# A graph network on one core: first-half ranks computed a stage earlier, keep ranks by quarters, and a halved first chain in the attention

## The chip, the cores and the metric

The program runs on one core of a Trainium2 chip. The metric is device time in microseconds (us). A core has TensorE (PE; its weight loads are PEld), VectorE (DVE), ScalarE (ACT), GpSimd (POOL) and SyncE (SP), whose queue issues the bulk DMAs. The engines run their own instruction streams and meet at semaphores.

## The reference

Eight graphs of 1024 nodes with 128 features pass through four residual blocks: an attention, a three-layer network on a thinned adjacency, a normalised graph convolution and a mask convolution. Each begins with a layer norm and a relu. Cut to what matters here:

```python
h = jnp.maximum(_layernorm(x, axis=-1), 0.0)
# attention
Wh = jnp.einsum('bnc,dc->bnd', h, W_w) + W_b
s = si[:, :, None] + sj[:, None, :] + a_b
e = jnp.exp(s) * A
h_prime = jnp.einsum('bij,bjc->bic', e / jnp.sum(e, axis=2, keepdims=True), h)
...
# thinning: row by row, a removal also clears the symmetric entry
def step(carry, n):
    row = jnp.take(carry, n, axis=0)
    nbi = row.astype(jnp.int32)
    num = jnp.sum(nbi)
    sf = jnp.where(num > T_DIL, (num + K_DIL - 1) // K_DIL, 1)
    rank = jnp.cumsum(nbi)
    rm = row & (rank % sf == 0)
    ...
    carry = carry.at[n].set(row & keep)
    carry = carry.at[:, n].set(carry[:, n] & keep)
...
# one layer on the thinned adjacency
agg = jnp.einsum('bij,bjd->bid', adj, x) / deg
out = agg @ Wr + x @ Wx + b
return out / nrm * mf[..., None]
```

## The kernel before, in words

A graph's nodes are cut into NB = 8 blocks of P = 128; HALF is 512 columns, one PSUM bank of f32. The stages follow one another with a barrier between: attention, removal, the fused stage, two layers, the convolution and the last block. The change touches the first three.

**Attention** (`attention_phase`, L173). Graph order is 1 to 7, then 0. Per graph: norm statistics on DVE (`mean`), the root on POOL (`root`), the scaled relu on ACT (`normalised`, L122), two score sums per block on DVE (`score_sums`, L415), the exponentials on ACT (`scores`, L363), the right-hand side on POOL (`right_hand_side`, L284) and 64 f32 products on PE (`attention`, L333), which waits for the right-hand side and for all four chunks of the adjacency. SP loads x of the first graph, waits for it, loads x of the second, then four 1 MB chunks per graph (L234). ACT issues five small constants itself; DVE waits for them first of all. ACT also sums every column of the adjacency (`column_sums`), DVE writes the bits into T8 (`bits`).

**Removal** (`removal_phase`, L488). All eight graphs go together, block by block. In block nb DVE runs 2 to 4 rounds (`parameters`, `hits`), each answered by PE (`lost`), then sets the removal parameters kd and kb (`far_parameters`). Beside these rounds the previous block is finished: PE forms its far ranks (`far_codes`, L629) in a ring of three PSUM slots, ACT turns them into distances (`distances`, L775 and L778), DVE compares them (`staying`, L907), PE and ACT form the current rows (`current`, L643, L787), PE counts them (`far_counts`, L586). DVE can't begin the next block before these counts (`pl_summed`, L926). After the last block ACT norms the first graph (L122), then forms the last distances, and DVE ends the stage with them (L911).

**Fused stage** (`fuse_phase`, L977). T8 is now final, and each graph is treated in 8 steps. A piece (nb, lo, hi) is up to 512 columns left of block nb's diagonal; a graph has 12. Per piece PE makes ranks (`ranks`, L1082: one fp8 matmul per block jb, from jb's column to the piece's end, so 512, 384, 256 and 128 columns for a full piece), ACT the distance to the bias kb (or kbhigh in the second half) (`distances`, L1192), DVE the removal bits into the buffer low (`removals`, L1271). Two rank banks alternate. With the bits, PE makes a mask per half row block (`masks`), DVE applies it to the adjacency (`masked_rows`, L1283), and PE adds the layer's f32 products (`sums`, L1143). In a step PE does the masks of graph b, the ranks of graph b+1, small projections, and the sums of the step before. The ranks of graph 0 come before the first mask, all 12 pieces one after the other.

## Time and profile before

| what | us |
|---|---|
| three runs | 1225.6, 1227.59, 1229.71; median 1227.59 |
| the profiled execution | 1230.29 |
| its span, first to last instruction | 1228.5 |
| PE busy | 1132.6 (92% of the span) |
| DVE busy | 768.1 (63%) |
| ACT busy | 603.2 (49%) |

The stages by their first and last instructions: attention ends with PE's products at 142.9 us, removal with DVE at 323.7 us, the fused stage begins on PE at 324.6 us. A timeline row gives start, duration, engine, line, the tile written and read, the count, and in brackets the idle time before it with what ended it. "issue" is a gap that no wait explains. PEclk is the clock that TensorE was granted, 1.00 being the upper level.

### The profile page before, as it was taken

The numbers are of one execution on the slowest core, as the hardware profiler recorded it, in microseconds if no ns is written. First come the engines' busy times: TensorE is split into PE (matmuls) and PEld (weight loads), VectorE is DVE, ScalarE is ACT, GpSimd is POOL, SyncE is SP. The second block draws the span as 40 slices with busy tenths as digits, with TensorE's granted clock in tenths as the row PEclk, the third lists the DMA queues.
The fourth block names the chain that finished last, engine by engine and source line by source line (L and its number), as shares of the span: only waits on it lengthen the run. The fifth ranks groups of instructions, "written<-read, shape, count | busy, mean of one in ns | idle before, by whom it ended". The sixth has DMA issues, their size and how long they took to land. (4 is left out here: it accounts for less than half of the span.)

```text
span 1228.5 us, 26838 instructions
## 1 busy us (share of the span) xinstructions
PE 1132.6 (92%) x9677; PEld 928.4 (76%) x9693; DVE 768.1 (63%) x2813; ACT 603.2 (49%) x1557; POOL 114.3 (9%) x129
## 2 busy tenths in 40 slices
PE   3999899998599999999899999999999899996998
PEld 3999866665388889889699999799999555543554
DVE  5899578677467777766434545435364655646973
ACT  3888557676746666664323334223435523314351
POOL 3333000000000000000000000213132101100000
PEclk9999889876699999999899999999999999998999
DMA  8977212110336677773246663157575355634911
GB/s 330 315 284 282 63 25 35 24 30 14 142 134 263 257 275 275 275 270 143 86 172 245 270 226 136 53 197 302 193 301 196 133 218 210 257 137 190 397 47 52
DMA packets 105513, 228.92 MB, mean 186 GB/s; under 512 B 34528, under 2 KB 53152, under 8 KB 105376
## 3 DMA queue, kind: packets, MB, share of 16 engines
q1 hardware_dynamic: 104656, 227.07, 50.0%
q8 instruction: 80, 1.31, 0.4%
q14 instruction: 57, 0.47, 0.1%
q10 hardware_dynamic: 720, 0.07, 0.0%
HBM read 185.70 MB, written 37.75 MB: 182 GB/s over the span
## 5 line engine op out<-in xcount | busy, mean ns | idle before, releaser
L1488 PE MATMUL lay_acc<-lay_z,k_keepadj 128*128 128x128 f32 x1024 | 117.0, 275 | 0.0
L1488 PE MATMUL lay_acc<-lay_z,k_otheradj 128*128 128x128 f32 x1024 | 117.0, 275 | 0.0
L1488 PEld LDWEIGHTS lay_acc<-lay_z,k_keepadj 128*128 128x128 f32 x1024 | 115.6, 192 | 0.0
L1488 PEld LDWEIGHTS lay_acc<-lay_z,k_otheradj 128*128 128x128 f32 x1024 | 115.6, 192 | 0.0
L1538 ACT ACTIVATE lay_junk<-lay_o 128x128 bf16<-128x128 f32 x128 | 37.7, 295 | 123.1 <-DVEq L1633 123.1
L1608 DVE TENSOR_TENSOR lay_o<-lay_ring,k_vec 128x512 f32<-128x512 f32 x32 | 22.1, 692 | 104.2 <-PE lay_ring L1481 104.2
L333 PE MATMUL att_acc<-att_rhs,att_adjT 128*128 128x130 f32 x512 | 60.8, 283 | 13.3 <-POOLq L285 12.3
L1587 POOL TENSOR_TENSOR lay_bl<-k_vec,k_mask 128x256 f32<-128x256 f32 x32 | 21.0, 655 | 553.6 <-DVEq L1623 549.7
L333 PEld LDWEIGHTS att_acc<-att_rhs,att_adjT 128*128 128x128 f32 x512 | 60.2, 198 | 13.8 <-POOLq L285 12.4
L1546 ACT ACTIVATE lay_o<-lay_o,lay_nrm 128x128 f32<-128x128 f32 x128 | 39.4, 388 | 54.4 <-DVE lay_nrm L1644 54.4
L1192 ACT ACTIVATE fuse_dist<-fuse_prank,k_kb 128x512 f16<-128x512 f32 (+2 forms) x64 | 38.9, 607 | 51.7 <-PE fuse_prank L1082 49.5
L1143 PE MATMUL fuse_acc<-fuse_z,k_otheradj 128*128 128x129 f32 x512 | 61.9, 275 | 0.0
L1143 PE MATMUL fuse_acc<-fuse_z,k_keepadj 128*128 128x129 f32 x512 | 61.9, 275 | 0.0
L333 PE MATMUL att_acc<-att_rhs,k_keepadj 128*128 128x130 f32 x512 | 58.1, 276 | 1.9 <-issue 1.9
L1143 PEld LDWEIGHTS fuse_acc<-fuse_z,k_keepadj 128*128 128x128 f32 x512 | 59.4, 192 | 0.0
L1143 PEld LDWEIGHTS fuse_acc<-fuse_z,k_otheradj 128*128 128x128 f32 x512 | 59.4, 192 | 0.0
L333 PEld LDWEIGHTS att_acc<-att_rhs,k_keepadj 128*128 128x128 f32 x512 | 57.5, 191 | 2.5 <-issue 2.5
L1283 DVE SCALAR_TENSOR_TENSOR k_otheradj<-fuse_pmask,k_otheradj 128x512 f32<-128x512 f32 x64 | 44.1, 689 | 21.5 <-PE fuse_pmask L1104 13.0
L1760 PE MATMUL gcn_agg<-k_keepadj,gcn_hs 128*128 128x512 f32 x128 | 56.4, 593 | 1.2 <-DVE k_keepadj L1857 1.2
L1082 PE MATMUL fuse_prank<-k_fore,k_T 128*128 128x128 fp8e5 (+3 forms) x288 | 46.5, 289 | 11.8 <-PEq L140 9.7
L1283 DVE SCALAR_TENSOR_TENSOR k_keepadj<-fuse_pmask,k_keepadj 128x512 f32<-128x512 f32 x64 | 44.1, 689 | 20.8 <-PE fuse_pmask L1104 10.8
L1760 PE MATMUL gcn_agg<-k_otheradj,gcn_hs 128*128 128x512 f32 x128 | 56.3, 592 | 0.0
(295 smaller groups left out, 2535.8 us busy)
## 6 DMA issues: line engine op xcount, KB each, us to landing
k_keepadj<-in_adj_cols SPq DMA_DIRECT2D x28, 1024.0 KB, 9.0
k_keepadj<-keptT SPq DMA_DIRECT2D x12, 2048.0 KB, 11.0
k_otheradj<-keptT SPq DMA_DIRECT2D x12, 2048.0 KB, 11.1
att_adjT<-in_adj_cols SPq DMA_DIRECT2D x16, 1024.0 KB, 8.1
k_otheradj<-in_adj_cols SPq DMA_DIRECT2D x16, 1024.0 KB, 10.3
keptT<-k_keepadj SPq DMA_DIRECT2D x16, 1024.0 KB, 4.6
keptT<-k_otheradj SPq DMA_DIRECT2D x16, 1024.0 KB, 4.6
lay_rowf<-in_adj_rows SPq DMA_DIRECT2D x32, 512.0 KB, 14.6
```

The costliest lines, as they stand in the source:

```text
L333: mm = t.matmul(acc[n % NA][:, e // 2, e % 2, 0:W], adjT[i % 2][:, jb, ib * P:(ib + 1) * P], rhs[i % 2][:, jb, 0:W], start=(jb == 0), stop ...
L1082: mm = t.matmul(prank[n % NR][:, a - lo:hi - lo], T8[:, b, jb, nb * P:(nb + 1) * P], K["fore8"][:, a - jb * P:hi - jb * P], start=(jb == f ...
L1143: mm = t.matmul(acc_tile(ib)[:, 0:ZW], adjT[b % 2][:, jb, ib * P:(ib + 1) * P], zz[:, jb, :], start=(jb == 0 and ib % 3 == 0), stop=(jb == ...
L1192: a.activation(dist[n % NR][:, 0:hi - lo], prank[n % NR][:, 0:hi - lo], ACT.Abs, bias=bias)
L1283: v.scalar_tensor_tensor(rows, pmask[n % NM][:], -0.5, rows, ALU.is_lt, ALU.mult)
L1488: mm = t.matmul(acc[i % 2][k][:, ib % HB, :], adjT[i % 2][:, jb, ib * P:(ib + 1) * P], zz[i % 2][:, jb, :], start=(jb == 0), stop=(jb == N ...
L1538: a.activation(junk[:, ib, :], o[i % 2][:, ib, :], ACT.Square, accum_out=nrm[:, 0, ib:ib + 1])
L1546: last = a.activation(o[i % 2][:, ib, :], o[i % 2][:, ib, :], ACT.Relu, scale=nrm[:, 4, ib:ib + 1])
L1587: g.tensor_tensor(bl[:], along_tiles(K["vec"][:, V_BL, :], 2), along_features(K["mask"][:, tile:tile + 2], D), ALU.mult)
L1608: v.tensor_tensor(o[i % 2][:, half * HB:(half + 1) * HB, :], ring[n % NS][:], along_tiles(K["vec"][:, V_B1 + layer, :], HB), ALU.add)
L1760: mm = t.matmul(agg[b % 2][:, sl], hs[b % 2][:, jb, :], adjT[b % 2][:, jb, sl], start=(jb == 0), stop=(jb == NB - 1))
```

## The change

- **Attention, first graph.** x comes in two halves with a semaphore each. SP then waits for the small constants, not for x, and x of the second graph goes behind the first graph's four adjacency chunks. DVE takes the statistics of the first half ahead of the constants. ACT signals the relu after four of eight blocks, and DVE's score sums begin there. The exponentials come ahead of the first column sums, and the first right-hand side is made by DVE.
- **Removal.** The pieces of graph 0 in the first half of blocks 0 to 6 (seven of its 12) are made here: `near_ranks` on PE at the end of a block, `near_distances` on ACT behind the current rows, `near_removals` on DVE two blocks later in round 0. `far_counts` keeps more partial counts. The norm of the first graph moves on ACT from the stage's end into block 0. 14 idle matmuls stand at PE's end.
- **Fused stage.** Each piece is ranked by quarters of 256 columns, each counted from its own start, so the widths are 256, 128, 256, 128. Each quarter has its own bias, and ACT does one activation per quarter. Graph 0 has five pieces left ahead of the first mask.
- **Memory.** low is kept for the whole program, and buffers of other stages are laid over it.

```diff
-                load_x(0)
-                sp.wait_ge(x_loaded[0], 16)
-                load_x(1)
+                for half in range(2):
+                    ts = slice(half * NB // 2, (half + 1) * NB // 2)
+                    sp.dma_start(x_rows(0)[:, ts, :], graph(A["x"], order[0])[:, ts, :]).then_inc(x_first[half], 16)
+                sp.wait_ge(small_loaded, 16 * 5)
                 for i in range(2):
                     for c in range(NC):
                         load_adjacency(i, c)
-                    load_x(i + 2)
-                for i in range(4, B):
+                    load_x(i + 1)
+                for i in range(3, B):
                     load_x(i)
                 sp.dma_start(maski[:], A["nodemask"].rearrange("b (t p) -> (b t) p", p=P)).then_inc(mask_loaded, 16)
...
-                root(0)
                 for i in range(B):
-                    right_hand_side(i)
-                    if i == 0:
-                        root(1)
-                    if 0 < i < B - 1:
-                        root(i + 1)
+                    root(i)
+                    if i > 0:
+                        right_hand_side(i)
...
+                normalised_first()
+                act.drain()
+                scores(0)
+                column_sums(0, 0)
...
-                    dve.wait_ge(h_ready, i + 1)
+                    dve.wait_ge(h_ready if i > 0 else half_ready, i + 1)
...
+                        if i == 0 and t == NB // 2:
+                            dve.wait_ge(h_ready, 1)
...
+                def first_rows():
+                    x = x_rows(0)
+                    for half in range(2):
+                        dve.wait_ge(x_first[half], 16)
+                        if half == 1:
+                            both_columns()
+                        for t in range(half * NB // 2, (half + 1) * NB // 2):
+                            v.bn_stats(w["part"][:, t, :], x[:, t, :])
+                    dve.drain()
+                    for t in range(NB):
+                        last = v.bn_aggr(w["pair"][:, t, :], w["part"][:, t, :])
+                    last.then_inc(w["mean_ready"], 1)
+
+                def first_right_hand_side():
+                    dve.wait_ge(exp_ready, 1)
+                    v.tensor_copy(rhs[0][:, :, D], E[0][:])
+                    v.tensor_tensor(rhs[0][:, :, 0:D], h[0][:], along_features(E[0][:], D), ALU.mult)
+                    dve.drain().then_inc(rhs_ready, 1)
...
+                def near_ranks(nb):
+
+                    o = take()
+                    top = min(HALF, (nb + 1) * P)
+                    for jb in range(min(nb, HALF // P - 1) + 1):
+                        mm = t.matmul(o[:, jb * P:top], T8[:, 0, jb, nb * P:(nb + 1) * P], K["fore8"][:, 0:top - jb * P],
+                                      start=(jb == 0), stop=(jb == min(nb, HALF // P - 1)))
+                    mm.then_inc(ring_ready, 1)
...
-                        if nb < LOW:
-                            for jb in range(LOW, NB):
-                                add(pl[:, NB + jb - LOW, b:b + 1], T8[:, b, nb, jb * P:(jb + 1) * P], K["ones8"][:, 0:1])
+                        beyond_pair = 2 * (nb // 2) + 2
+                        for jb in range(beyond_pair, NB):
+                            slot_of = LOWSLOT + {2: 0, 4: 6, 6: 10}[beyond_pair] + jb - beyond_pair
+                            add(pl[:, slot_of, b:b + 1], T8[:, b, nb, jb * P:(jb + 1) * P], K["ones8"][:, 0:1])
...
+                    if not more:
+                        keep_busy(t, K, take()[:, 0:HALF], 14)
...
+                def near_distances(nb):
+
+                    if nb >= 2:
+                        act.wait_ge(near_read, nb - 1)
+                    o = take()
+                    top = min(HALF, (nb + 1) * P)
+                    a.activation(near_dist[nb % 2][:, 0:top], o[:, 0:top], ACT.Abs, bias=K["kb"][:, nb:nb + 1])
+                    act.drain().then_inc(near_ready, 1)
+                    act.sem_inc(ring_free, 1)
...
+                        near_distances(prev)
+                    else:
+                        norm_apply(nc, act, lambda t: K["X"][:, t, :], K["h"][:], row, 0, first_h)
                     if more:
                         distances(nb, first)
-                norm_apply(nc, act, lambda t: K["X"][:, t, :], K["h"][:], row, 0, first_h)
                 distances(NB - 1, range(B))
...
+                def near_removals(nb):
+
+                    dve.wait_ge(near_ready, nb + 1)
+                    top, c0 = min(HALF, (nb + 1) * P), low_columns(nb)
+                    v.tensor_scalar(K["low"][:, c0:c0 + top], near_dist[nb % 2][:, 0:top], K["kd"][:, nb:nb + 1], None, ALU.is_equal)\
+                        .then_inc(near_read, 1)
...
+                        if nb > 1 and k == 0:
+                            near_removals(nb - 2)
...
-                high = K["kb"][:].rearrange("p (b t) -> p t b", t=NB)[:, LOW:NB, :]
-                v.tensor_tensor(K["kbhigh"][:], high, lowcount[:], ALU.add)
+                kb = K["kb"][:].rearrange("p (b t) -> p t b", t=NB)
+                sides = K["rdeg"][:].rearrange("p (b t) -> p t b", t=NB)
+                v.tensor_tensor(lowcount[:, 6:10, :], lowcount[:, 6:10, :], lowcount[:, 2:6, :], ALU.add)
+                v.tensor_tensor(sides[:, 0:6, :], kb[:, 2:8, :], lowcount[:, 0:6, :], ALU.add)
+                dve.drain()
+                v.tensor_tensor(lowcount[:, 10:12, :], lowcount[:, 10:12, :], lowcount[:, 8:10, :], ALU.add)
+                v.tensor_tensor(K["kbhigh"][:], kb[:, LOW:NB, :], lowcount[:, 6:10, :], ALU.add)
+                dve.drain()
+                v.tensor_tensor(sides[:, 6:8, :], kb[:, 6:8, :], lowcount[:, 10:12, :], ALU.add)
+                near_removals(NB - 2)
                 staying(NB - 1, range(B))
...
+    early = [q for q in range(NP) if pieces[q][0] < NB - 1 and pieces[q][1] == 0]
+    left = [q for q in range(NP) if q not in early]
...
+        def of_block(b, nb):
+            return [q for q in (left if b == 0 else range(NP)) if pieces[q][0] == nb]
+
+        def piece_number(b, q):
+            return left.index(q) if b == 0 else b * NP + q - len(early)
+
+        def quarters(lo, hi):
+            return [(q0, min(q0 + HALF // 2, hi)) for q0 in range(lo, hi, HALF // 2)]
+
+        def offset(b, nb, q0):
+
+            t = b * NB + nb
+            if q0 == HALF:
+                return K["kbhigh"][:, nb - NB // 2, b:b + 1]
+            return {0: K["kb"][:, t:t + 1], HALF // 2: K["rdeg"][:, t - 2:t - 1] if nb >= 2 else None,
+                    3 * HALF // 2: K["rdeg"][:, t:t + 1]}[q0]
 
         def acc_tile(ib):
...
-                        for jb in range(first_jb, last_jb + 1):
-                            a = max(jb * P, lo)
-                            mm = t.matmul(prank[n % NR][:, a - lo:hi - lo], T8[:, b, jb, nb * P:(nb + 1) * P],
-                                          K["fore8"][:, a - jb * P:hi - jb * P], start=(jb == first_jb), stop=(jb == last_jb))
+                        for q0, q1 in quarters(lo, hi):
+                            for jb in range(q0 // P, q1 // P):
+                                mm = t.matmul(prank[n % NR][:, jb * P - lo:q1 - lo], T8[:, b, jb, nb * P:(nb + 1) * P],
+                                              K["fore8"][:, 0:q1 - jb * P], start=(jb * P == q0), stop=((jb + 1) * P == q1),
+                                              skip_group_check=True)
...
+                ranks(0, 4)
                 side_work("turn_h", 0, 0)
-                ranks(0, 1)
+                ranks(0, 5)
                 side_work("turn_h", 0, 1)
-                ranks(0, 2)
-                ranks(0, 3)
+                ranks(0, 6)
+                ranks(0, 7)
                 side_work("z", 0, 0)
-                for nb in range(4, NB):
-                    ranks(0, nb)
                 for b in range(B + 1):
                     if b < B:
...
                         tile = b * NB + nb
-                        bias = K["kb"][:, tile:tile + 1] if lo == 0 else K["kbhigh"][:, nb - NB // 2, b:b + 1]
-                        a.activation(dist[n % NR][:, 0:hi - lo], prank[n % NR][:, 0:hi - lo], ACT.Abs, bias=bias)
+                        for q0, q1 in quarters(lo, hi):
+                            a.activation(dist[n % NR][:, q0 - lo:q1 - lo], prank[n % NR][:, q0 - lo:q1 - lo], ACT.Abs,
+                                         bias=offset(b, nb, q0))
                         act.drain().then_inc(dist_ready, 1)
 
                 def side_copy(kind, b, half):
```

In all three of the following places names are those of the program; k_low is the buffer low, att_sj the scores, att_rhs the right-hand side. First DVE at the start of the attention, before:

```order
L445 COPY att_abc<-att_acol 128x128 x2
L92 BN_STATS att_n_part<-k_X 128x6 x8
L95 BN_AGGR att_n_pair<-att_n_part 128x2 x8
L400 SCALAR_TENSOR_TENSOR att_n_stat<-att_n_stat,att_n_pair 128x8
L450 COPY att_av<-att_pset 128x256
L451 COPY att_ac<-att_pset 128x2
L453 TENSOR_TENSOR att_ac<-att_ac,att_ab 128x1
L415 SCALAR_TENSOR_TENSOR att_prod,att_sj<-att_h,att_av 128x128 x16
L92 BN_STATS att_n_part<-k_X 128x6 x8
```

and in the change:

```order
L440 BN_STATS att_n_part<-k_X 128x6 x4
L430 COPY att_abc<-att_acol 128x128 x2
L440 BN_STATS att_n_part<-k_X 128x6 x4
L443 BN_AGGR att_n_pair<-att_n_part 128x2 x8
L406 SCALAR_TENSOR_TENSOR att_n_stat<-att_n_stat,att_n_pair 128x8
L479 COPY att_av<-att_pset 128x256
L480 COPY att_ac<-att_pset 128x2
L482 TENSOR_TENSOR att_ac<-att_ac,att_ab 128x1
L423 SCALAR_TENSOR_TENSOR k_low,att_sj<-att_h,att_av 128x128 x16
L448 COPY att_rhs<-att_E 128x8
L449 TENSOR_TENSOR att_rhs<-att_h,att_E 128x8x128
L92 BN_STATS att_n_part<-k_X 128x6 x8
```

Four of the statistics stand ahead of the copies of the constants, and the right-hand side stands ahead of the second graph's statistics. Next ACT from the end of the removal stage to the first distances of the fused stage, before:

```order
L787 ACTIVATE k_T<-rem_ring,rem_minus 128x256 x8
L122 ACTIVATE k_h<-k_X,rem_n_stat 128x128 x8
L775 ACTIVATE rem_dist<-rem_cand,rem_shift 128x128 x8
L561 UNCONDITIONAL_BRANCH
L1176 UNCONDITIONAL_BRANCH
L1231 ACTIVATE fuse_prime<-k_eps 128x1
L1192 ACTIVATE fuse_dist<-fuse_prank,k_kb 128x128
L1202 ACTIVATE fuse_hT<-fuse_misc 128x512
L1192 ACTIVATE fuse_dist<-fuse_prank,k_kb 128x256
L1202 ACTIVATE fuse_hT<-fuse_misc 128x512
L1192 ACTIVATE fuse_dist<-fuse_prank,k_kb 128x384
L1192 ACTIVATE fuse_dist<-fuse_prank,k_kb 128x512
```

and in the change:

```order
L837 ACTIVATE k_T<-rem_ring,rem_minus 128x256 x8
L847 ACTIVATE rem_near_dist<-rem_ring,k_kb 128x512
L825 ACTIVATE rem_dist<-rem_cand,rem_shift 128x128 x8
...
L1285 ACTIVATE fuse_dist<-fuse_prank,k_kbhigh 128x128
L1296 ACTIVATE fuse_hT<-fuse_misc 128x512
L1285 ACTIVATE fuse_dist<-fuse_prank,k_kbhigh 128x256
L1296 ACTIVATE fuse_hT<-fuse_misc 128x512
L1285 ACTIVATE fuse_dist<-fuse_prank,k_kbhigh 128x256
L1285 ACTIVATE fuse_dist<-fuse_prank,k_rdeg 128x128
L1285 ACTIVATE fuse_dist<-fuse_prank,k_kb 128x256
L1285 ACTIVATE fuse_dist<-fuse_prank,k_rdeg 128x256
```

The eight norm activations have left the end, one distance has come in their place, and the fused stage begins with the second-half piece of block 4; k_rdeg holds the biases of the second and fourth quarter. Last PE in step 7 of a graph, where two full pieces are ranked, before:

```order
L1082 MATMUL fuse_prank<-k_fore,k_T 128x512
L1082 MATMUL fuse_prank<-k_fore,k_T 128x384
L1082 MATMUL fuse_prank<-k_fore,k_T 128x256
L1082 MATMUL fuse_prank<-k_fore,k_T 128x128
L1082 MATMUL fuse_prank<-k_fore,k_T 128x512
L1082 MATMUL fuse_prank<-k_fore,k_T 128x384
L1082 MATMUL fuse_prank<-k_fore,k_T 128x256
L1082 MATMUL fuse_prank<-k_fore,k_T 128x128
L1130 MATMUL fuse_misc<-k_Wr,fuse_hT 128x128 x4
```

and in the change:

```order
L1176 MATMUL fuse_prank<-k_fore,k_T 128x256
L1176 MATMUL fuse_prank<-k_fore,k_T 128x128
L1176 MATMUL fuse_prank<-k_fore,k_T 128x256
L1176 MATMUL fuse_prank<-k_fore,k_T 128x128
L1176 MATMUL fuse_prank<-k_fore,k_T 128x256
L1176 MATMUL fuse_prank<-k_fore,k_T 128x128
L1176 MATMUL fuse_prank<-k_fore,k_T 128x256
L1176 MATMUL fuse_prank<-k_fore,k_T 128x128
L1225 MATMUL fuse_misc<-k_Wr,fuse_hT 128x128 x4
```

The count stays at eight matmuls, the columns go from 2560 to 1536.

## Rows read from the trace of the kernel before

**Rows 1.** the profile page, part 1: busy us (share of the span), instructions

```profile
PE 1132.6 (92%) x9677; PEld 928.4 (76%) x9693; DVE 768.1 (63%) x2813; ACT 603.2 (49%) x1557; POOL 114.3 (9%) x129
```

**Rows 2.** window of 32 us: busy of PE, PEld, DVE, ACT, POOL, then PEclk

```profile
377.00:409.00 32.00, 31.63 (x305) 28.67 (x306) 23.54 (x67) 20.70 (x57) 0.00 (x0) 1.00 0.69 260
```

**Rows 3.** timeline of PE: start us, us, engine, line, what; fused stage, step 7

```profile
394.97 0.39 PE L1107 MATMUL fuse_pmask<-k_minus,k_T 128*128 128x128 fp8e5 x4
395.19 0.22 PE L1095 MATMUL fuse_pmask<-k_T,k_minus 128*128 128x128 fp8e5 x1
...
395.69 1.25 PE L1082 MATMUL fuse_prank<-k_fore,k_T 128*128 128x512 fp8e5 x8
396.78 0.44 PE L1130 MATMUL fuse_misc<-k_Wr,fuse_hT 128*128 128x128 f32 x2
```

**Rows 4.** waits in total, times, longest (us): PE in 345 to 600 us

```profile
PE fuse_pmask L1095 <- issue: 1.9, 7, 0.3
```

**Rows 5.** groups by line and shape, ACT: xcount, then busy, mean ns, idle

```profile
L1192 ACT ACTIVATE fuse_dist<-fuse_prank,k_kb 128x512 f16<-128x512 f32 x35 | 24.1, 688 | 42.8 <-PE fuse_prank L1082 42.8
...
L1192 ACT ACTIVATE fuse_dist<-fuse_prank,k_kbhigh 128x256 f16<-128x256 f32 x7 | 3.3, 474 | 1.1 <-issue 1.1
```

**Rows 6.** timeline of PE, start of the fused stage

```profile
324.56 0.27 PE L1082 MATMUL fuse_prank<-k_fore,k_T 128*128 128x128 fp8e5 x1 [9.74 <-PEq L140]
...
338.24 0.39 PE L1095 MATMUL fuse_pmask<-k_T,k_minus 128*128 128x512 fp8e5 x1 [1.63 <-DVE fuse_low L1271]
```

**Rows 7.** window (columns as in rows 2), entry of the fused stage

```profile
324.00:329.00 5.00, 4.04 (x18) 2.84 (x19) 0.58 (x3) 2.82 (x6) 0.11 (x1) 0.50 0.67 220
```

**Rows 8.** timeline of ACT, end of the removal stage

```profile
316.28 3.18 ACT L122 ACTIVATE k_h<-k_X,rem_n_stat 128x128 f32<-128x128 f32 x8 [0.26 <-issue]
319.37 3.90 ACT L775 ACTIVATE rem_dist<-rem_cand,rem_shift 128x128 f16<-128x128 f16 x8
```

**Rows 9.** timeline of DVE, the same place

```profile
319.81 0.35 DVE L911 SCALAR_TENSOR_TENSOR k_T<-rem_dist,k_kd,k_T 128x128 fp8e5<-128x128 f16 x1 [3.70 <-ACTq L780]
```

**Rows 10.** timeline of PE, attention's first products

```profile
20.52 17.25 PE L333 MATMUL att_acc<-att_rhs,att_adjT 128*128 128x130 f32 x128 [12.29 <-POOLq L285]
38.23 14.53 PE L333 MATMUL att_acc<-att_rhs,k_keepadj 128*128 128x130 f32 x128 [0.45 <-issue]
```

**Rows 11.** timeline of all engines, start of attention

```profile
5.61 2.11 SPq L234 DMA_DIRECT2D att_adjT<-in_adj_cols  x4
5.95 0.36 DVE L445 COPY att_abc<-att_acol 128x128 f32<-128x128 f32 x2 [5.95 <-DMA att_ab<-in_L_gnn_a_b]
6.23 1.64 DVE L92 BATCH_NORM_STATS2 att_n_part<-k_X 128x6 f32<-128x128 f32 x8
...
12.61 1.63 ACT L122 ACTIVATE att_h<-k_X,att_n_stat 128x128 f32<-128x128 f32 x4
14.27 0.29 DVE L415 SCALAR_TENSOR_TENSOR att_prod<-att_h,att_av 128x128 bf16<-128x128 f32 x1 [2.71 <-ACT att_h L122]
...
18.52 1.90 POOL L284 TENSOR_TENSOR att_rhs<-att_h,att_E 128x1024 f32<-128x1024 f32 x1
...
30.47 1.90 POOL L284 TENSOR_TENSOR att_rhs<-att_h,att_E 128x1024 f32<-128x1024 f32 x1
```

**Rows 12.** DMA, 0 to 60 us in 40 slices

```profile
GB/s 0 73 313 10 144 372 407 415 423 426 415 426 349 378 404 404 410 407 421 401 326 293 295 296 289 290 301 425 423 401 421 421 412 101 0 19 246 412 421 418
```

**Rows 13.** waits of DVE, removal stage, 166 to 300 us

```profile
DVE rem_stays L907 <- ACTq L780: 7.8, 13, 1.3
DVE rem_w L926 <- PEq L732: 7.2, 4, 2.4
```

**Rows 14.** timeline of PE, removal stage, end of block 4

```profile
262.57 0.49 PE L586 MATMUL rem_pl<-k_ones,k_T 128*128 128x1 fp8e5 x14
263.69 0.33 PE L586 MATMUL rem_pl<-k_ones,k_T 128*128 128x1 fp8e5 x7 [0.62 <-ACTq L789]
```

**Rows 15.** groups by line and shape, DVE in 345 to 600 us

```profile
L1271 DVE TENSOR_SCALAR fuse_low<-fuse_dist,k_kd 128x512 bf16<-128x512 f16 x42 | 14.8, 353 | 9.3 <-ACTq L1193 6.5
```

120 lines of the change are left out of this document (63 added, 57 removed).

## The prediction

> **What bounds the kernel now.** I read the page first: PE is busy for 92% of the span, DVE for 63%, ACT for 49% [rows 1]. That share is a mean over stages, so each stage the change touches was read for what ends its waits last.
>
> *Fused stage.* In a window of 32 us, one graph's work, PE is busy for 31.6, DVE for 23.5 and ACT for 20.7, at granted clock 1.00 [rows 2]. In all of 345 to 600 us PE waits 1.9 us in front of the masks [rows 4]. So what PE sheds is shed from the stage. Its matmuls go by their columns: in step 7 the eight rank matmuls, 2 x (512+384+256+128) = 2560 columns, stand from 395.69 to 396.78, 1.09 us, and four of 128 columns with changing weights from 394.97 to 395.19, 0.055 each [rows 3]. That is 0.0533 per 128 columns at the upper level, 2.4 GHz.
>
> *Entry of the fused stage.* From PE's first rank to the first mask pass 338.24 - 324.56 = 13.7 us, and the mask was released by DVE's removal bits, the end of the chain PE, ACT, DVE over 12 pieces [rows 6]. Until 329 PE is granted 0.50, 1.2 GHz [rows 7].
>
> *End of removal.* ACT norms for 3.18 us from 316.28 and only then starts the last distances, at 319.37 [rows 8]; DVE had waited 3.70 us for them [rows 9].
>
> *Inside removal* no engine is full. DVE waits 7.8 us for ACT's distances and 7.2 for PE's counts [rows 13]. Here the change adds work to all three.
>
> *Start of attention.* PE waits 12.29 us for POOL's right-hand side, until 20.52 [rows 10]. The chain there is constants, statistics, root, relu, score sums, exponentials, right-hand side [rows 11]. The next product starts at 38.23, after a gap of 0.45 that no other engine ends [rows 10]; from there PE is the bound, so an earlier first product moves the stage's end.
>
> **The change, part by part.**
>
> *Ranks by quarters.* A piece of m blocks had m(m+1)/2 units of 128 columns. Full pieces (six per graph) go from 10 units to 6, pieces of three (two) from 6 to 4, the rest stay. 80 units become 52, so 28 x 0.0533 = 1.49 us per graph, and 7 x 1.49 = 10.4 us for graphs 1 to 7, whose ranks stand in PE's full steps. Graph 0 is in the next term. For it ACT pays one more activation in eight pieces: 512 columns take 688 ns, 256 take 474 [rows 5], so 2 x 474 - 688 = 260 ns, 2.1 us per graph: ACT goes from 20.7 to 22.8 of then 30.5 us. Work of PE hides it; if that cover failed, up to 2.1 x 7 = 15 us would come back, more than the gain. I take it as hidden: two rank banks give a piece a whole step to be read, and a step has 3.8 us. DVE's work stays. Gain 10.4; bounds 0 (ACT's latency eats all of it) and 10.4.
>
> The Trainium skill, "TensorE: Matmul & The Clock Gate", section "Back-to-back issue gap", puts a sustained stream of weight load and matmul at about 81 ns per matmul of 128 columns, since the load counts too. That would speak against quarters: the 128-column matmuls of a graph go from 12 to 20, and the gain would be an estimated 8 x 0.027 x 7 = 1.5 us smaller. The trace has 55 ns for the same pair [rows 3], so the trace decides, and the sum goes by columns.
>
> *Graph 0's first halves made early.* Of 12 pieces 5 remain ahead of the first mask: 128, 256, 384, 512 and 512 columns. ACT's line there, by the durations of rows 5 (107 ns per 128 columns above 260): 0.37 + 0.47 + 0.84 + 0.95 + 0.95 = 3.6 us, and the two copies of hT, each taken as a full activation, 0.69: 5.0 together. Eight gaps of 0.16 to 0.2 between them, from the idle before such groups, 7 x 0.16 = 1.1 in total [rows 5], add 1.4; start 0.3, the last removal and its hand-over 0.5. Sum 7.2 against 13.7: gain 6.5. The end norm root and z copy now stand behind the last distance, not ahead of it. Bounds: 5 (if PE's half clock makes it wait between) and 8.
>
> *The norm off the end.* It goes to block 0, where ACT has nothing until the first parameters. At the end ACT runs one near distance, 0.69 + 0.18, in its place: 3.18 - 0.87 = 2.3 us earlier. DVE's five small sums and a near removal fit in the 3.70 it waited [rows 9]. Gain 2.3; bounds 1.5 and 3.1. What is late next is the same chain of eight distances. The 14 matmuls of PE behind it are 14 x 0.213 at full and 0.427 at half clock, 3 to 6 us, starting near 315.5, so they end by 321.5, about when DVE ends; at worst they cost 0.5. They keep PE occupied up to the stage change.
>
> *What removal pays.* Seven near ranks, distances and removals, and 64 more one-column counts. DVE: a 512-wide removal takes 353 ns [rows 15], narrower ones less, six of them in round 0 of blocks 2 to 7, 1.6 to 1.9 us; nothing of DVE's own hides them, only its waits for ACT. PE: the counts and the near ranks stand ahead of the signal on which DVE starts a block. 14 counts take 0.49 [rows 14], 0.03 each. At the end of blocks 1 and 2, where PE comes last, ten counts and one or three short ranks cost about 0.45 each, 0.9. Later PE waits 0.62 there for ACT's rows [rows 14], which covers four rank matmuls (10 units, 0.53). ACT: near distances of 0.87 delay the next block's distances, which wait for PE's far ranks anyway early on; for blocks 5 and 6 I count 1.4. Queued behind ACT's near distance are three far distances, and DVE's `staying` waits for those. Sum 3.9, less 0.8 where DVE's removal falls into a wait for ACT: 3.1 lost. Bounds: 0, since more work on PE may hold its clock up, and all additions in a row: 1.9 for DVE, 4.7 for ACT (0.55 + 0.65 + 0.76 + 3 x 0.87 rounded up for hand-overs), 40 units at half clock 4.3, 64 counts 1.8: 12.7.
>
> *Attention.* Four of eight statistics go ahead of the constants, half of 1.64: 0.8. Score sums start after four of eight relus: the last four take 1.63 [rows 11], so 1.6. The right-hand side takes POOL 1.90 [rows 11]; on DVE, not shown here, it is bound by three widths of rows 15 (f16 in) and POOL's own 1.9; I take 1.2, gain 0.6. The chain gives 3.0. But PE also needs the last adjacency chunk. Counted by slices of 1.5 us [rows 12], 5.2 MB have arrived by about 18.5. Without the 0.5 MB of the second x, at 415 GB/s, this is 1.3 earlier, and 0.35 later because SP now starts at 5.95 and not at 5.61 [rows 11]. So the chunk lands at 17.6 and the rest of the hand-over makes 18.0: gain 2.5. The second x arrives at about 19, which delays DVE by about 1 us; the second product, wanted at 35.7, had its right-hand side at 32.4 [rows 11], so 2 us of cover are left. Bounds 0.5 and 3.2. The warm-up of PE (17.25 against 14.53 [rows 10]) stays.
>
> *Sum.* -10.4 - 6.5 - 2.3 + 3.1 - 2.5 = -18.6 us. The profiled execution is 1230.3 (span 1228.5 and 1.8 around it), so 1211.7; it lies 2.7 above the median of the runs. Against the median 1227.6 this is 1209.0, the forecast.
>
> **The rivals.**
>
> *A: the quarters' gain stays on paper.* ACT's longer chain reaches the graph's boundary, where the first mask waits for all bits of the next graph. For: DVE already waits for ACT there 6.5 us in full pieces [rows 15]. Against: ACT waits for PE 42.8 us in front of these activations [rows 5], and behind the last ranks PE still has 16 sums. If half of the 10.4 is lost, the time is 1214; if all, 1219.
>
> *B: removal pays in full.* ACT is last in most blocks and the three-slot ring passes each near rank's delay on. For: the waits of DVE [rows 13]. Against: those of PE for ACT [rows 14]. 12.7 instead of 3.1 gives 1218.
>
> *C: slower.* The near rank takes a ring slot at each block's end, PE stands blocked until ACT frees one, and its granted clock stays at 0.50 for the rest of removal, as it is at the stage's end. It decides from about 22 us lost there, 3.2 per block, nearly twice what all additions come to in a block at their upper bound (12.7 over seven). The time would be 1231. Nothing in the rows shows such a wait.
>
> *D: the early pieces don't shorten the entry*, because the transposes and projections alone take it. They take PE and ACT together under 5 us, so at most 2 us are lost: 1211. Within the forecast's range.
>
> **How the numbers follow.** Forecast with D 0.74, A 0.10, B 0.12, C 0.04. The forecast's own bounds (attention 0.5 to 3.2, entry 5 to 8, end 1.5 to 3.1, removal 0 to 5) give 1203 to 1215. The range reaches into A and B: 1202 to 1218. This kernel's runs tell about 0.3%, 3.7 us, from no change. Faster by more than that 0.94, within it 0.03, slower 0.03.
>
> **What would show it.** Right: a graph's stretch in the fused stage falls from about 32 us to 30.6 with PE still without waits; the first mask comes 7 us behind the first rank; the last distances begin right behind the near distance; PE's first product starts near 18; removal between attention's end and its own last distance is about 3 us longer. Wrong: PE waits for removal bits at graph boundaries (A), DVE's waits for counts and distances above 20 us (B), or a mean clock in removal clearly below before (C).

## The result, and the profile after

| | before | after |
|---|---|---|
| median of the timed runs, us | 1226.99 (1225.60 to 1229.71) | 1211.94 (1209.21 to 1214.89) |
| ratio, 95% interval | | 0.9871, 0.9848 to 0.9894 |
| profiled execution, us | 1230.29 | 1211.67 |
| its span, mean granted clock | 1228.5, 0.954 | 1209.9, 0.967 |

The change saves 15.1 us of the median, 18.6 of the profiled execution. The forecast was 1209.0 with a range of 1202 to 1218: the time lies inside, 2.9 above the forecast. The sum of the prediction was -18.6, exactly what the two profiles differ by. That is luck, since its terms were not right, and their errors cancel. One run of one experiment, 1913.7 us at a granted clock of 0.558 in the kernel with one activation, is left out everywhere below. This is how the spans divide, each mark read from the same instruction in both profiles:

| stretch | before | after | difference | in the sum |
|---|---|---|---|---|
| start to the end of attention's products | 142.9 | 145.9 | +3.0 | -2.5 |
| from there to the fused stage's first rank | 181.7 | 178.6 | -3.1 | +0.8 (3.1 - 2.3) |
| first rank to first mask | 13.7 | 6.6 | -7.1 | -6.5 |
| first mask to the 26 filling matmuls behind the last graph | 250.1 | 241.4 | -8.7 | -10.4 |
| from there to the end | 640.2 | 637.5 | -2.7 | 0 |

One term was close (the entry), one was a fifth too large, two had the wrong sign, and one was missing.

The page of the changed kernel, part 1 (busy us, share of the span, instructions); before in [rows 1]:

```profile
PE 1118.8 (92%) x9755; PEld 925.1 (76%) x9771; DVE 769.9 (64%) x2819; ACT 612.2 (51%) x1616; POOL 112.9 (9%) x127
```

**Attention.** The timeline of PE (start, us, engine, line, operation; in brackets what it idled for), the changed kernel; before in [rows 10]:

```profile
18.36 15.99 PE L331 MATMUL att_acc<-att_rhs,att_adjT 128*128 128x130 f32 x128 [10.24 <-DMA att_adjT<-in_adj_cols]
34.71 14.53 PE L331 MATMUL att_acc<-att_rhs,k_keepadj 128*128 128x130 f32 x128 [0.36 <-POOLq L286]
53.52 17.15 PE L331 MATMUL att_acc<-att_rhs,att_adjT 128*128 128x130 f32 x128 [4.28 <-DMA att_adjT<-in_adj_cols]
71.14 14.53 PE L331 MATMUL att_acc<-att_rhs,k_keepadj 128*128 128x130 f32 x128 [0.47 <-issue]
```

The first product starts 2.2 us earlier than before, about as forecast (18.4; forecast near 18), and the second 3.5 earlier. Then the third waits 4.28 us for its adjacency and, after the pause, takes 17.15 instead of 14.53. In the wait the mean granted clock is 0.83, in the first 2.5 us of the product 0.50. The third product starts at 53.52, 0.3 behind the 53.23 of the kernel before, so the early start is given back by the wait, and 2.6 of the 3.0 us lost are the slower product. DVE's statistics, ACT's relus and SP's issues of the changed kernel show why:

```profile
20.02 1.65 DVE L92 BATCH_NORM_STATS2 att_n_part<-k_X 128x6 f32<-128x128 f32 x8 [2.90 <-DMA k_X<-in_x]
33.20 1.64 DVE L92 BATCH_NORM_STATS2 att_n_part<-k_X 128x6 f32<-128x128 f32 x8 [1.62 <-DMA k_X<-in_x]
```

```profile
40.07 3.19 ACT L122 ACTIVATE att_h<-k_X,att_n_stat 128x128 f32<-128x128 f32 x8 [3.20 <-DVE att_n_stat L406]
43.16 1.04 ACT L378 ACTIVATE k_low<-att_adjT 128x1024 bf16<-128x1024 f32 x1
```

```profile
17.59 18.91 SPq L230 DMA_DIRECT2D k_X<-in_x  x6
36.54 2.02 SPq L247 DMA_DIRECT2D att_maski<-in_nodemask  x1
38.69 7.29 SPq L234 DMA_DIRECT2D att_adjT<-in_adj_cols  x4
```

The second graph's x is now behind 4 MB of adjacency, so DVE's second statistics start at 20.02 instead of 17.95; the third's wait again. ACT, which takes graphs in turn, does the third graph's relus at 40.07 (before: 36.83) and only behind them the column sums of the last chunk of the first graph's buffer, from 43.16. On these SP waits before it issues the last chunk of the third graph's adjacency into that buffer, at 45.61 instead of 42.67.

This delay is real, but it is not all that PE waits for. The rate of the DMA in the changed kernel, 30 to 60 us in 40 slices of 0.75 us:

```profile
GB/s 324 287 295 295 292 289 279 298 292 293 289 272 304 273 205 382 378 404 421 410 404 404 426 421 377 399 421 399 317 366 377 333 229 333 410 399 437 415 410 273
```

From 41.25 to 51 us it never pauses: while the last chunk wasn't issued, the three ahead of it were still moving. It landed 7.7 us behind its issue, at 53.3. In the kernel before it landed 8.7 us behind its issue, at 51.4, and PE, still in its second product until 52.76, didn't see it. So a third product could not have started much before 51.4 even with the old order, and an earlier start of PE can give at most about 2 us there. The prediction has no term for this.

**End of removal, and entry of the fused stage.** ACT and PE there, the changed kernel; before in [rows 6, 8]:

```profile
318.32 0.69 ACT L847 ACTIVATE rem_near_dist<-rem_ring,k_kb 128x512 f16<-128x512 f32 x1 [0.37 <-PE rem_ring L689]
319.24 3.92 ACT L825 ACTIVATE rem_dist<-rem_cand,rem_shift 128x128 f16<-128x128 f16 x8 [0.24 <-issue]
```

```profile
318.14 3.26 PE L1459 MATMUL rem_ring<-k_fore,k_ident 128*128 128x512 fp8e5 x14
324.47 0.22 PE L1176 MATMUL fuse_prank<-k_fore,k_T 128*128 128x128 fp8e5 x1 [3.07 <-PEq L140]
328.61 0.82 PE L1176 MATMUL fuse_prank<-k_fore,k_T 128*128 128x256 fp8e5 x4 [0.55 <-ACTq L1287]
331.04 0.63 PE L1190 MATMUL fuse_pmask<-k_T,k_minus 128*128 128x512 fp8e5 x1
```

The last distances stand right behind the near one, and the first mask comes 6.6 us behind the first rank with no wait of its own (before, 1.63).

**Fused stage.** A window of one graph, 30.8 us (columns as in [rows 2]), and the waits of PE in 345 to 570 us (engine, line, whom it waited for: total us, times, longest):

```profile
394.90:425.70 30.80, 30.44 (x307) 28.46 (x307) 23.72 (x67) 22.13 (x65) 0.00 (x0) 1.00 0.72 273
```

```profile
PE fuse_pmask L1190 <- issue: 2.0, 7, 0.3
PE fuse_misc L1223 <- ACT fuse_o L1322: 0.2, 1, 0.2
```

PE is still the bound, with waits as in [rows 4]; ACT went from 20.7 in 32 us to 22.1 in 30.8.

**Behind the fused stage**, in code that the change leaves as it is, PE gets its clock back sooner. Windows of 3 us (the number behind POOL is the granted clock) at the same place, 15 us behind the start of the filling matmuls, before and after:

```profile
603.30:606.30 3.00, 3.00 (x13) 2.35 (x12) 0.84 (x2) 0.00 (x0) 0.00 (x0) 0.50 0.97 388
```

```profile
587.40:590.40 3.00, 3.00 (x23) 2.50 (x22) 0.64 (x2) 0.78 (x2) 0.00 (x0) 0.90 1.02 401
```

At 0.50 (the 1.2 GHz level) 13 matmuls start, at 0.90 23. In windows of 1.5 us from the same start, the clock is back at 1.00 some 2.5 us sooner. The second layer begins (first 2 us) at 0.56 before and 1.00 after, the convolution at 0.50 and 1.00. The first layer is 1.1 us shorter, the second 0.8, the rest 0.8.

### The profile page after: what moved, and what is told of

Same layout as the page of the kernel before. It is cut to its first block and busy times, and to the rows that moved or that the text cites. A ratio compares the mean times of both kernels' runs of the same rounds, so it can differ in the third digit from the quotient of the medians.

```text
span 1209.9 us, 27058 instructions
## 1 busy us (share of the span) xinstructions
PE 1118.8 (92%) x9755; PEld 925.1 (76%) x9771; DVE 769.9 (64%) x2819; ACT 612.2 (51%) x1616; POOL 112.9 (9%) x127
## 5 line engine op out<-in xcount | busy, mean ns | idle before, releaser
L1701 DVE TENSOR_TENSOR lay_o<-lay_ring,k_vec 128x512 f32<-128x512 f32 x32 | 22.1, 692 | 102.4 <-PE lay_ring L1574 102.4
L331 PE MATMUL att_acc<-att_rhs,att_adjT 128*128 128x130 f32 x512 | 62.2, 287 | 15.1 <-DMA att_adjT<-in_adj_cols 14.5
L1680 POOL TENSOR_TENSOR k_low<-k_vec,k_mask 128x256 f32<-128x256 f32 x32 | 21.2, 664 | 535.4 <-DVEq L1716 531.9
L666 PE MATMUL rem_ring<-k_back,k_T 128*128 128x512 fp8e5 (+3 forms) x272 | 51.0, 350 | 2.9 <-ACTq L829 1.9
L2109 PE MATMUL l_agg<-k_T,k_low 128*128 128x512 fp8e5 x192 | 44.5, 394 | 9.4 <-PEq L140 9.4
```

What stands on the lines that cost most here:

```text
L331: mm = t.matmul(acc[n % NA][:, e // 2, e % 2, 0:W], adjT[i % 2][:, jb, ib * P:(ib + 1) * P], rhs[i % 2][:, jb, 0:W], start=(jb == 0), stop ...
L666: mm = t.matmul(o[:, lo - f0:top - f0], T8[:, b, mb, n0:n0 + P], K["back8"][:, u0:u0 + top - lo], start=(mb == NB - 1), stop=(mb == lo // P))
L1680: g.tensor_tensor(bl, along_tiles(K["vec"][:, V_BL, :], 2), along_features(K["mask"][:, tile:tile + 2], D), ALU.mult)
L1701: v.tensor_tensor(o[i % 2][:, half * HB:(half + 1) * HB, :], ring[n % NS][:], along_tiles(K["vec"][:, V_B1 + layer, :], HB), ALU.add)
L2109: mm = t.matmul(agg[b % 2][:, sl], parts[b % 2][:, q, jb, :], bits_of(b, jb)[:, sl], start=(jb == 0 and q == 0), stop=(jb == NB - 1 and q ...
```

## Experiments

Each set of runs has the kernel before beside it on the same chip (the sets were on different chips); the ratio is to that kernel, with its 95% interval in brackets, so between sets compare the ratios. The marks are of one profile each. "Removal" is the stretch from the end of attention's products to the first rank.

| kernel | median us | ratio | attention's end | removal | entry | fused |
|---|---|---|---|---|---|---|
| changed | 1211.9 | 0.9871 [0.9848, 0.9894] | 145.9 | 178.6 | 6.6 | 241.4 |
| changed, again | 1210.5 | 0.9861 [0.9839, 0.9883] | 145.2 | 178.7 | 6.6 | 241.3 |
| old attention | 1209.2 | 0.9859 [0.9839, 0.9880] | 142.0 | 179.0 | 6.7 | 240.7 |
| second x first | 1207.8 | 0.9848 [0.9826, 0.9870] | 142.0 | 179.5 | 6.8 | 241.0 |
| loads by need | 1208.3 | 0.9830 [0.9788, 0.9872] | 141.5 | 180.5 | 6.7 | 240.9 |
| both moves | 1208.9 | 0.9850 [0.9828, 0.9872] | 143.1 | 179.7 | 6.8 | 240.8 |
| whole ranks | 1221.3 | 0.9950 [0.9931, 0.9968] | 146.9 | 179.2 | 6.3 | 250.0 |
| one activation | 1211.1 | 0.9873 [0.9847, 0.9899] | 143.9 | 178.7 | 6.3 | 239.8 |
| norm only | 1223.0 | 0.9956 [0.9933, 0.9980] | 142.6 | 174.6 | 13.6 | 250.0 |
| no fill | 1211.7 | 0.9856 [0.9801, 0.9911] | 145.9 | 178.8 | 7.0 | 240.9 |
| no near pieces | 1209.7 | 0.9846 [0.9803, 0.9889] | 143.0 | 177.1 | 6.1 | 240.7 |
| norm at the end | 1214.4 | 0.9895 [0.9874, 0.9915] | 145.2 | 180.7 | 7.0 | 241.2 |
| before, again | 1230.9 (one run) | | 143.2 | 181.9 | 13.7 | 250.1 |

### Attention: the old stage

The changed kernel with the attention functions of the kernel before (buffers shared as in the changed one):

```diff
-                first_rows()
+                dve.wait_ge(small_loaded, 16 * 5)
+                for half in range(2):
+                    last = v.tensor_copy(abc[:, half, :], acol[:, half:half + 1].to_broadcast([P, P]))
+                last.then_inc(abc_ready, 1)
+                mean(0)
...
-                first_right_hand_side()
```

> The changed kernel with the attention stage of the kernel before. My theory: the new attention costs 3.0 us instead of gaining 2.5, because the second graph's x now lands behind 4 MB of adjacency, DVE's second statistics start 2 us late, and with them every step of the chain up to the adjacency chunks of the third graph. So PE ends the stage at 142.9 us as before (145.9 in the changed kernel), the third product starts without a wait and lasts 14.5, and the time falls by 3.0, to about 1209. Rival: the stage's end merely varied between the two profiles, and the new attention is a gain of 2: then the time is about 1214.

The stage ends at 142.0 and the median falls by 2.8 against the first set of the changed kernel, by 1.3 against the second. The ratios (0.9859 against 0.9871 and 0.9861) don't tell them apart; the stage's end does. PE's first and third products of this kernel:

```profile
20.59 16.38 PE L331 MATMUL att_acc<-att_rhs,att_adjT 128*128 128x130 f32 x128 [12.29 <-POOLq L283]
52.34 14.53 PE L331 MATMUL att_acc<-att_rhs,att_adjT 128*128 128x130 f32 x128 [0.48 <-DVEq L439]
```

With the first product 2.2 us later, the third starts 1.2 earlier. The changed kernel, profiled again, waits 3.30 us at its third product, which takes 16.18, and ends the stage at 145.2, as was expected of it. Over seven profiles with the new attention the stage ends between 143.0 and 146.9 (median 145.2), over four with the old one (the before kernels' included) between 142.0 and 143.2 (median 142.7). The ranges touch, and the medians are 2.5 apart: the new attention is a loss in most profiles, not in all. The one at 143.0 (no near pieces) tells where the loss sits:

```profile
53.27 14.53 PE L331 MATMUL att_acc<-att_rhs,att_adjT 128*128 128x130 f32 x128 [2.46 <-DMA att_adjT<-in_adj_cols]
```

It waits 2.46 us, the granted clock stays at 1.00, and the product takes 14.53. In the six others PE waited 2.89 to 4.48 us, the product took 16.18 to 17.29, and the stage ended at 143.9 or later. What is lost is the slower product.

### Attention: the second graph's x first

```diff
                 sp.wait_ge(small_loaded, 16 * 5)
+                load_x(1)
                 for i in range(2):
                     for c in range(NC):
                         load_adjacency(i, c)
-                    load_x(i + 1)
+                    load_x(i + 2)
```

> The changed kernel with one transfer moved: the second graph's x is issued ahead of the first adjacency. My theory (late x): the first product starts about 1 us later, at 19.4, the second right-hand side is ready by 33 and not 34.2, the third product starts at 51.5 to 52 with no wait for its adjacency and lasts 14.5, and the stage ends near 142; the time falls by 4, to about 1208. Rival (ACT's new order): the column sums come late because ACT now runs exponentials, column sums and relus of the second graph in another order, so the third product still waits some 4 us for its last chunk and the stage ends at 146 or 147: time 1212 to 1213.

DVE's second statistics and PE's products in it:

```profile
17.24 1.65 DVE L92 BATCH_NORM_STATS2 att_n_part<-k_X 128x6 f32<-128x128 f32 x8 [0.19 <-issue]
```

```profile
19.69 17.00 PE L332 MATMUL att_acc<-att_rhs,att_adjT 128*128 128x130 f32 x128 [11.65 <-DMA att_adjT<-in_adj_cols]
37.05 14.53 PE L332 MATMUL att_acc<-att_rhs,k_keepadj 128*128 128x130 f32 x128 [0.36 <-issue]
52.20 14.53 PE L332 MATMUL att_acc<-att_rhs,att_adjT 128*128 128x130 f32 x128 [0.62 <-DMA att_adjT<-in_adj_cols]
```

The wait for x is gone, the third product starts at 52.20 after 0.62 us, at full speed, and the stage ends at 142.0. ACT's order is the changed one, so that rival falls: the place of one 0.5 MB transfer decides. The time, 1207.8, is as expected.

The way there is not only the theory's. The wait of 4.28 us is 3.66 shorter. Of these, 2.34 come from PE, whose second product ends at 51.58 and not at 49.24, since the first one starts later and takes longer. Only 1.3 come from the adjacency: its last chunk is issued 4.2 us sooner, at 41.45, but lands 10.5 behind its issue, at 52.0.

### Attention: loads in the order of need

```diff
                 for i in range(2):
                     for c in range(NC):
                         load_adjacency(i, c)
-                    load_x(i + 1)
-                for i in range(3, B):
-                    load_x(i)
-                sp.dma_start(maski[:], ...)
+                    if i == 0:
+                        load_x(1)
+                        load_x(2)
+                load_x(3)
                 for i in range(2, B):
...
                         load_adjacency(i, c)
+                    if i + 2 < B:
+                        load_x(i + 2)
+                    if i == 2:
+                        sp.dma_start(maski[:], ...)
```

> The changed kernel with SP's loads in the order of need: x of the first two following graphs behind the first adjacency, x of the fourth behind the second, the rest and the node mask behind the third adjacency and later. The first product keeps its early start. My theory (what is late in the changed kernel is the third graph's adjacency, which SP issues only at 38.7 us, behind six loads of x and the mask, and whose last chunk waits for the late column sums): first product at 18.3, second at 34.8, third at about 50 without a cold clock, stage's end near 140, so 6 us earlier than the 145.9 of the changed kernel and 2 earlier than with the second x first; time about 1206. Rival: the order of SP's queue is worth nothing since the late x of the second graph alone sets the chain; then the third product still starts at 52 to 53.5, the end is 144 to 146 and the time 1210 to 1212.

```profile
18.23 16.31 PE L335 MATMUL att_acc<-att_rhs,att_adjT 128*128 128x130 f32 x128 [10.26 <-DMA att_adjT<-in_adj_cols]
35.07 14.56 PE L335 MATMUL att_acc<-att_rhs,k_keepadj 128*128 128x130 f32 x128 [0.54 <-POOLq L290]
50.20 14.55 PE L335 MATMUL att_acc<-att_rhs,att_adjT 128*128 128x130 f32 x128 [0.57 <-POOLq L290]
65.33 14.54 PE L335 MATMUL att_acc<-att_rhs,k_keepadj 128*128 128x130 f32 x128 [0.58 <-POOLq L290]
```

SP's row of this kernel for the third graph's adjacency starts at 34.61 instead of 38.69, and the third product at 50.20, as the theory said. Here the second x is still late, ACT's relus for the third graph come at 39.44 and the last chunk is issued at 44.98, nearly as late as in the changed kernel; yet it lands 5.0 us later: the three ahead of it had been moved by 44.5, where the DMA's rate falls to nothing. So the late column sums alone don't make the wait of 4.28 us; the place of this adjacency behind six loads of x and the mask has part in it. But the stage ends at 141.5, not 140, and the time is 1208.3, not 1206: five products now wait 0.54 to 0.58 for POOL's right-hand side, at a spacing of 15.1 us, and the last one 1.74, 4.5 us in all. DVE's late x had hidden behind the late adjacency; with that gone, the chain through DVE, ACT and POOL is the bound.

### Attention: both moves together

> The changed kernel with both moves of SP's loads: the second graph's x ahead of the first adjacency, and the later graphs' x and the mask behind the third adjacency. Theory (behind the third product DVE's period of 15.1 us per graph and PE's 15.0 leave nothing to gain): the first product starts at 19.5 to 19.7, the third at 51.8 to 52 without a wait, the stage ends at 141.5 to 142, and the time is 1207.5, 4.5 under the changed kernel and the same as either move alone. Rival (the two moves add): the stage ends at 140 and the time is 1205.5.

It is 1208.9, against 1210.5 for the changed kernel beside it; 1207.5 was expected. The moves don't add, as expected. The stage ended at 143.1, not 141.5 to 142: in this profile the first product waited for its adjacency until 20.88, 1.2 longer than in the kernel with one move, and everything behind kept this distance. The second x first, alone, is the version with the lowest median, 1207.8 us (0.9848); loads by need, at 1208.3, can't be told from it.

### Fused stage: ranks whole again

```diff
-                        for q0, q1 in quarters(lo, hi):
-                            for jb in range(q0 // P, q1 // P):
-                                mm = t.matmul(prank[n % NR][:, jb * P - lo:q1 - lo], ...
+                        for jb in range(lo // P, hi // P):
+                            mm = t.matmul(prank[n % NR][:, jb * P - lo:hi - lo], ...
...
-                        for q0, q1 in quarters(lo, hi):
-                            a.activation(dist[n % NR][:, q0 - lo:q1 - lo], ...
+                        a.activation(dist[n % NR][:, 0:hi - lo], ...
```

> The changed kernel with the fused stage's ranks whole again and one activation per piece (for the pieces from block 2 on in each half the second half then lacks the quarters' offset only if ranks were by quarters; here none is missing). My theory: PE's columns set the graph's stretch, so it goes from 30.75 back to 32.1 to 32.3 us, the entry gets longer by at most 0.5, and the time rises by 7 x 1.4 = 10, to about 1222. Rival: part of the 1.37 per graph came from a better standing between DVE and PE after the early pieces; then whole ranks give 31.5 and the time is 1217.

The spacing of the graphs, by DVE's first instruction on each graph's row sums (changed kernel, then this one):

```profile
395.16 0.17 DVE L1387 TENSOR_SCALAR k_rdeg<-fuse_summed 128x8 f32<-128x8 f32 x1
425.89 0.17 DVE L1387 TENSOR_SCALAR k_rdeg<-fuse_summed 128x8 f32<-128x8 f32 x1
```

```profile
398.66 0.17 DVE L1383 TENSOR_SCALAR k_rdeg<-fuse_summed 128x8 f32<-128x8 f32 x1
430.78 0.17 DVE L1383 TENSOR_SCALAR k_rdeg<-fuse_summed 128x8 f32<-128x8 f32 x1
```

30.73 against 32.12, and 32.12 is the kernel before's spacing to the hundredth. The stretch from the first mask is 250.0, again as before. So the quarters alone make this gain: 8.7 to 9.3 us by profiles (250.0 against 240.7 to 241.4 in the nine profiles with the same fused code) and 9.3 to 10.8 by medians. The rival is out. The early pieces keep their own gain: the first mask still comes 6.3 behind the first rank.

### Fused stage: one activation

```diff
-                        for q0, q1 in quarters(lo, hi):
-                            a.activation(dist[n % NR][:, q0 - lo:q1 - lo], prank[n % NR][:, q0 - lo:q1 - lo], ACT.Abs,
-                                         bias=offset(b, nb, q0))
+                        a.activation(dist[n % NR][:, 0:hi - lo], prank[n % NR][:, 0:hi - lo], ACT.Abs, bias=offset(b, nb, lo))
```

> The changed kernel, ranks by quarters, but one activation per piece with the first quarter's offset (leaves out the second offset). It sizes the 2.1 us that ACT got per graph. My theory: they lie beside PE's work, ACT idles longer in front of them, the graph's stretch stays at 30.75 within 0.1 and the entry gets shorter by 0.5 to 0.9: time 1211.5 within 1. Rival: the 0.12 us per graph that the gain of 1.37 lacks against 1.49 are ACT's; then the stretch is 30.6 and the time about 1210.3.

```profile
392.18 0.17 DVE L1385 TENSOR_SCALAR k_rdeg<-fuse_summed 128x8 f32<-128x8 f32 x1
422.81 0.17 DVE L1385 TENSOR_SCALAR k_rdeg<-fuse_summed 128x8 f32<-128x8 f32 x1
```

The spacing is 30.63: 32.12 - 30.63 = 1.49, the columns' price per graph just as worked out. From the first mask it is 239.8, 10.2 below whole ranks (sum: 10.4), and 1.6 below the changed kernel. But the eight other profiles of the changed fused stage have 240.7 to 241.3 there, so ACT's second activation costs 0.9 to 1.6, where the sum had nothing. Between these two rows it is 0.10. The rival names it rightly. The entry is 6.3, 0.3 shorter, not 0.5 to 0.9. The median says nothing here: 1211.1 from runs of 1207.8 to 1213.0; 1 to 1.6 us is what these runs don't resolve.

### Removal: the norm moved, alone

The kernel before with one move:

```diff
                         current(prev, third)
+                    else:
+                        norm_apply(nc, act, lambda t: K["X"][:, t, :], K["h"][:], row, 0, first_h)
                     if more:
                         distances(nb, first)
-                norm_apply(nc, act, lambda t: K["X"][:, t, :], K["h"][:], row, 0, first_h)
                 distances(NB - 1, range(B))
```

> The kernel before with one move: the norm that ACT runs at the end of the removal goes to its block 0. From the attention's end to the first rank the kernel before takes 181.7 us, the changed one 178.6, where my sum had 182.5. Theory N: the norm alone is worth about 3.1 (all of its 3.18, since DVE and PE were waiting), so the stretch is 178.6 and the additions of the changed kernel cost nothing: time about 1223.6 against 1226.7. Theory C (clock): the norm gives the 2.3 to 3.1 but the additions cost 3, paid back by a higher granted clock; then this kernel has the stretch of 178.6 to 179.4 too, but the kernel without the near pieces (next run) is faster still. Rival P: the profile of the kernel before was a slow one in this stage; then the stretch is below 177.5.

The stretch is 174.6, 7.1 below, far more than the norm's 3.18: neither N nor C said so, and P's limit (below 177.5) is met. The median, 1223.0, is what N had (1223.6), for another reason. It is 4.7 below that of the kernel before beside it (1227.7), 3 to 4 below those of the other sets. The windows of the whole stretch, before and here:

```profile
142.90:324.56 181.66, 150.29 (x2146) 105.05 (x2146) 131.60 (x720) 119.66 (x217) 0.04 (x1) 0.78 0.14 23
```

```profile
142.60:317.15 174.55, 144.60 (x2144) 102.39 (x2145) 131.14 (x720) 119.66 (x217) 0.04 (x1) 0.82 0.15 24
```

DVE, ACT and the number of PE's matmuls are the same. PE's busy time falls by 5.7 us for the same matmuls, at a granted clock of 0.82 against 0.78. The last distances of this kernel, at the stage's end (before in [rows 8]):

```profile
311.95 3.92 ACT L775 ACTIVATE rem_dist<-rem_cand,rem_shift 128x128 f16<-128x128 f16 x8 [0.24 <-issue]
```

This splits the 7.1. Counted from the end of attention's products, ACT comes to the norm at 173.4 before, and to these distances at 169.4 here: 4.0 us are gained ahead of the place from which the norm was taken. The norm itself gives the other 3.1. The 4.0 don't fall in block 0, where the norm now stands. DVE's step behind the counts (L926 before, L927 here) comes, by the same count, at 51.7, 76.3, 100.9, 122.3, 142.3 and 160.3 before and at 51.4, 75.9, 99.4, 119.3, 139.1 and 156.3 here: most is gained between 76 and 122 us. The windows there, before and here:

```profile
243.80:264.00 20.20, 19.27 (x271) 13.88 (x271) 14.73 (x79) 14.92 (x24) 0.00 (x0) 0.83 0.18 28
```

```profile
239.60:259.00 19.40, 17.25 (x286) 13.04 (x283) 14.56 (x80) 15.33 (x25) 0.00 (x0) 1.00 0.19 30
```

The granted clock is 0.83 and 1.00. Why a move in block 0 changes it there wasn't found.

### Removal: the kernel before, again

> The kernel before, unchanged, for a second profile of it. In the first one PE was granted 0.78 from the attention's end to the first rank, and that stretch took 181.7 us; with the norm moved alone it took 174.5 at 0.82, 7.2 less, where the norm itself is 3.2 long. Theory C (the clock varies from run to run): a second profile of the kernel before has 178 to 180 in this stretch at 0.80 to 0.83, and the norm alone is then worth about 4. Rival: it has 181.5 to 182 again at 0.78, and moving the norm is worth 7 because PE's shorter idle time lets the clock recover. The stages behind it should repeat within 1 us.

The rival is right on the numbers: 181.9 at 0.78 once more, and all stages behind it repeat within 0.1 us. But this profiled execution, 1230.9, is again one of the longer ones. The timed runs of the kernel before lie in two groups. Over 37 of them, in the three sets of experiments (one more, at 1242, left out; of the four runs beside the result, which have no clock on record, one at 1226.4 lies between the groups), 18 have a granted clock of 0.954 to 0.957 and 1227.5 to 1231.1 us (median 1229.9), and 19 have 0.959 to 0.962 and 1224.8 to 1226.0 (median 1225.4). Both profiles are of the first group. The norm moved alone has 0.962 to 0.965 in eleven of twelve runs. Against the second group it is worth 2.4 us, near the norm's own 3.1 (the sum's 2.3 has a near distance taken off, which this kernel doesn't run). The 4.5 between the groups are close to the 4.0 gained ahead of the norm's place. That these are the same us, and that both profiles of the kernel before are its longer kind, is a reading that fits, but no profile of the second group was had. The rival's cause, a shorter idle time of PE, isn't shown either: the clock differs in the middle of the stage, not behind the norm.

### Removal: the norm back at the end

```diff
                         near_distances(prev)
-                    else:
-                        norm_apply(nc, act, lambda t: K["X"][:, t, :], K["h"][:], row, 0, first_h)
                     if more:
                         distances(nb, first)
+                norm_apply(nc, act, lambda t: K["X"][:, t, :], K["h"][:], row, 0, first_h)
                 distances(NB - 1, range(B))
```

> The changed kernel with the norm back at the end of the removal, ahead of the last distances. It is the fourth corner of a square: neither (kernel before, 181.7 us from the attention's end to the first rank), norm moved alone (174.5), both (178.6 to 180.5 in six profiles), additions alone (this one). Theory: the norm is worth 3 to 4 here too, the additions cost 2 to 5 with or without it: the stretch is 182 to 184 and the time 3 to 4 above the changed kernel, about 1215.5. Rival (the first profile's 181.7 is what the clock makes of it, and additions hold it up): additions alone leave 180 to 181.7 and the time is within 1.5 of 1212.

The stretch is 180.7, 2.0 above the changed kernel's, and the median 3.9 above its second set. The theory's 182 to 184 didn't come; the rival's 180 to 181.7 did, but not its time (within 1.5 of 1212; it is 1214.4). The fourth corner of the square closes it, and it is no square of costs that add. Without the additions the norm's move is worth 7.1 in the profiles; with them, 2.0. The additions cost 4.1 where the norm is moved already (174.6 to 178.7) and gain 1.0 where it isn't (181.7 to 180.7).

Divided at the point where ACT begins its last tasks (near distance, norm, last distances, as far as a kernel has them), the end does add. ACT at the end of this kernel:

```profile
316.62 0.69 ACT L847 ACTIVATE rem_near_dist<-rem_ring,k_kb 128x512 f16<-128x512 f32 x1 [0.38 <-PE rem_ring L689]
317.57 3.18 ACT L122 ACTIVATE k_h<-k_X,rem_n_stat 128x128 f32<-128x128 f32 x8 [0.26 <-issue]
320.66 3.90 ACT L825 ACTIVATE rem_dist<-rem_cand,rem_shift 128x128 f16<-128x128 f16 x8
```

| us | attention's end to ACT's last tasks | from there to the first rank |
|---|---|---|
| before | 173.4 | 8.3 |
| norm moved | 169.4 | 5.2 |
| additions | 171.4 | 9.3 |
| both | 172.4 | 6.2 |

In the last column the norm is worth 3.1 and the near distance costs 1.0, each time. In the first, the additions cost 3.0 with the norm moved and gain 2.0 without. The granted clock is 0.78 in the kernel before, 0.82 with the norm moved, 0.85 with the additions, 0.87 with both:

```profile
145.20:325.87 180.67, 151.95 (x2246) 106.77 (x2246) 133.73 (x732) 123.00 (x224) 0.04 (x1) 0.85 0.14 23
```

```profile
145.90:324.47 178.57, 152.37 (x2244) 106.47 (x2245) 133.79 (x731) 123.53 (x224) 0.04 (x1) 0.87 0.14 23
```

With both, PE executes 100 more matmuls than before and is busy only 2 us longer; against the norm moved alone it is busy 7.8 longer.

### Removal: no near pieces

```diff
                             far_counts(prev, second)
-                            near_ranks(prev)
...
-                        near_distances(prev)
...
-                        if nb > 1 and k == 0:
-                            near_removals(nb - 2)
```

> The changed kernel with the near ranks, their distances and removals taken out of the removal stage (so graph 0's first-half bits are never made; the 64 additional counts and the moved norm stay). My sum had 3.1 us for all additions. Theory C (clock): attention's end to the first rank, 178.6, falls by less than 0.5 or even rises, because the added matmuls hold PE's granted clock up. Theory S (my sum): it falls by 2.5, to 176, and the time to about 1209.5. Rival: they cost nothing because they stand in waits; then the stretch is the same within 0.5 at the same granted clock.

The stretch is 177.1 at a clock of 0.82, so the near pieces cost 1.6 there (1.5 to 3.4 by the other profiles of this stage, which lie between 178.6 and 180.5), and 0.8 to 2.2 us of the median. Theory C's "less than 0.5" is out; the 2.5 of my sum lies in that spread. The rest of the 4.1, 2.5 from 174.6 to 177.1, goes to the counts, the five sums and the fill together; they weren't told apart.

### Removal: no fill

```diff
-                    if not more:
-                        keep_busy(t, K, take()[:, 0:HALF], 14)
```

> The changed kernel without the 14 matmuls that PE runs behind its last counts of the removal. Theory: they are off the path there and keep the granted clock up into the fused stage's entry; without them the first rank comes at the same time within 0.3 and the entry (first rank to first mask, 6.6 us) gets 0.3 to 1.0 longer by slower ranks and transposes; time within 1 of 1212. Rival: they hold up the flag at the stage's end, and without them the time falls by 1 or more.

The first rank comes at 324.68 (324.47), the entry takes 7.0 instead of 6.6, and the time is 1211.7: as expected, nothing that a time shows (seven profiles of the same entry with the fill have 6.6 to 7.0). Behind the fused stage, though, this profile has 640.7 us and not 637.5.

## Why the prediction was right or wrong

**Direction and size**: right, with errors that cancelled, so the size is luck in part. Rivals A, B, C and D didn't come. PE has no new wait at graph boundaries (A). DVE's waits for distances and counts are 6.5 and 8.9 us between 145 and 300, below the 20 of B. The clock in removal is above before, not below (C). Of the signs named for being right, four came; "removal between attention's end and its own last distance is about 3 us longer" didn't: it is 3.1 shorter (176.5 before, 173.4 after).

**Quarters, -10.4**: the columns' term is right (10.2 shown with one activation, 1.49 per graph). The step that was mis-sized is "I take it as hidden": ACT's second activation costs 0.9 to 1.6 us of the 15 it could have. Net 8.7 to 9.3. The trace's 0.055 us per matmul of 128 columns held. The 81 ns that the Trainium skill gives ("TensorE: Matmul & The Clock Gate", section "Back-to-back issue gap") would have made it 1.3 per graph, an estimate; the trace shows 1.49.

**Early pieces, -6.5**: 7.1 by profile, 6.6 us from first rank to first mask for the 7.2 worked out. No run took the early pieces back alone; with whole ranks, and the early pieces kept, the entry stays at 6.3.

**Norm, -2.3, and what removal pays, +3.1**: both terms are near what the square shows, and yet the stretch is 3.1 us shorter where they make it 0.8 longer. The norm is worth 3.1 at the stage's end and the near distance in its place costs 1.0, net 2.1. Ahead of that, the additions cost 3.0 with the norm moved. The step that failed was to price both in work and waits alone: with either the norm moved or the additions in, the part ahead of ACT's last tasks takes 4.0 or 2.0 us less than in the kernel before, and the sum has nothing for it. The prediction listed "more work on PE may hold its clock up" as a reason for a bound of 0, and had the granted clock of 0.50 behind the stage in [rows 7], but gave no term to it. The clock over the stretch is 0.87 instead of 0.78 in the profile after. That the clock makes the 4.0 goes with the windows of the norm moved alone (0.83 and 1.00), but what sets it stays open, and so does whether a shorter run of the kernel before has the 4.0 already.

**Attention, -2.5**: the wrong sign, +3.0 (2.5 between medians of the profiles). The steps up to the first product were right: chunk and right-hand side ready for a start at 18.4, DVE's right-hand side 1.22 for the 1.2 taken. The failed step is "from there PE is the bound, so an earlier first product moves the stage's end", together with the look at the late x, which stops at the second product ("2 us of cover are left"). The x came at 20 and DVE was 2.1 late, not 1, but the cover held: the second product started 0.36 behind the first, a gap that other profiles show with no wait for POOL. The sum has no term for the third graph's adjacency, which in the kernel before landed at 51.4, 1.8 us ahead of the third product. PE, 3.5 us early, waited for it, until 53.5 since it also landed 1.9 later, and the clock fell: 2.6 us more in the product. That one transfer moved ahead takes the loss away is shown. How much of the later landing is the delay through DVE and ACT, and how much the order of the queue, isn't: in the kernel with loads by need the same delay costs PE no wait.

**Not in the sum**: 2.7 us behind the fused stage, where the granted clock returned some 2.5 us sooner. The changed code isn't there. In seven profiles (the changed kernel twice, and those that differ in the attention or in the norm's place) the stretch is 637.4 to 637.6; in the kernels without fill, without near pieces, with one activation and with whole ranks it is 639.1 to 640.7, in the kernel before 640.2 and 640.3, with the norm moved alone 640.0. What decides it wasn't found.

**The median**: the forecast took the sum off the median of all runs, 1227.6, but the sum was made against a profile of the longer group, 1230.3. If removal's 3.1 belong to that group, they can't be had again from a run of 1225.4. This is the likeliest cause of the 2.9 by which the time is above the forecast; it isn't shown.

## What to carry to other kernels

When an engine is made to start earlier, look up when its next inputs land, and not only the first: here the third adjacency, not the second product's right-hand side, was the limit, and waiting for it cost more than the start had gained. A forecast from one profile should ask to which clock that profile belongs before its sum is taken off the median. And divide a stage before calling its prices unstable: the same move was worth 7 us or 2, but 3.1 of either at the place where it was made, and the rest moved in a part that the edit doesn't touch.

## What was not expected of the hardware

The same program's timed runs lie in two groups by granted clock (0.954 to 0.957: 1229.9 us; 0.959 to 0.962: 1225.4), with a gap of 1.5 us between them. Six waits of PE of 2.89 to 4.48 us in the attention were each followed by a product of 16.18 to 17.29 us, where 14.53 is usual (1.7 to 2.8 more); after one wait of 2.46 us, in the same code, the granted clock stayed at 1.00 and the product took 14.53. And identical code behind the fused stage took 637.5 or 640.2 us, 2.7 apart, by when the clock came back.
